# A six-stage decoder on one core: the first batch's memory attention moved into the last two expert units, with its loads and GpSimd's order rearranged

## What is computed

```python
# third sublayer (L0 ffn): 8 experts, capacity 1024 rows each
h = _rms(buf, norm_w[:, None, :])
gate = gelu(einsum('ech,ehf->ecf', h, Wg)); up = einsum('ech,ehf->ecf', h, Wu)
buf_out = einsum('ecf,efh->ech', gate * up, Wd) + buf
combined = x + contrib.reshape(N, TOP_K, H).sum(axis=1)      # or fout where a token overflows
...
# fourth sublayer (L1 attn), the "memory attention": M = 64
q, k, v = x @ Wq, x @ Wk, x @ Wv
gates = sigmoid(x @ Wg + bg)
S = decay * S + (k_t * g_t)[:, :, None] * (v_t * g_t)[:, None, :]
out_t = einsum('bd,bde->be', q_t, S);   y = outs @ Wo + bo
...
# fifth (L1 xattn): softmax attention over ctx_1024 with a mask; sixth (L1 ffn): 8 experts, all dense
```

## Time and profile before

| | us |
|---|---|
| Median of three runs | 1936.16 (1933.49 to 1940.54) |
| Profiled execution | 1936.2, span of its instructions 1934.4 |
| Mean granted TensorE clock, share of 2.4 GHz | 0.972 |
| TensorE busy | 1778.2 (92%) |
| VectorE, ScalarE, GpSimd busy | 1261.8, 991.2, 640.9 |

### The profile page before, as it was taken

One profiled execution on the slowest core, in us unless ns is written; L12 is line 12 of the kernel. 1 busy time (PEld: TensorE's weight loads), 2 busy tenths in 40 slices (PEclk: granted clock), 3 DMA queues, 4 the chain that ended last, 5 costly groups with the idle time before them and its releaser, 6 DMA issues. The chain is left out here.

```text
span 1934.4 us, 26137 instructions
## 1 busy us (share of the span) xinstructions
PE 1778.2 (92%) x8373; PEld 1056.8 (55%) x8373; DVE 1261.8 (65%) x2933; ACT 991.2 (51%) x2603; POOL 640.9 (33%) x821
## 2 busy tenths in 40 slices
PE   7999878899999898989889999999689999999997
PEld 5556534455555554545456556655455666566553
DVE  2686568898899999898411211221576878786665
ACT  4336699999999999896231111111242333233220
POOL 2000055555767676675410001000442323212100
PEclk9999989999999999999899999999788999999999
DMA  6248831122223222223653443332311111200000
GB/s 218 101 158 280 260 94 53 53 65 68 80 65 96 65 75 86 62 80 129 206 173 109 127 145 131 109 127 97 115 58 41 55 39 49 49 12 17 11 12 22
DMA packets 164072, 183.29 MB, mean 95 GB/s; under 512 B 19653, under 2 KB 143804, under 8 KB 162913
## 3 DMA queue, kind: packets, MB, share of 16 engines
q1 hardware_dynamic: 157792, 165.46, 27.0%
q0 software_dynamic: 6144, 16.18, 2.7%
HBM read 119.01 MB, written 63.18 MB: 94 GB/s over the span
## 5 line engine op out<-in xcount | busy, mean ns | idle before, releaser
L914 POOL TENSOR_SCALAR xa_probs<-xa_probs,xa_small 128x512 f32<-128x512 f32 x512 | 345.1, 691 | 227.6 <-DVE xa_small L1078 227.5
L987 ACT ACTIVATE xa_probs<-xa_ps_s,xa_small 128x512 f32<-128x512 f32 x512 | 363.6, 752 | 23.8 <-DVE xa_small L1084 20.1
L1084 DVE TENSOR_REDUCE xa_small<-xa_ps_s 128x2 f32<-128x1024 f32 x256 | 309.2, 1208 | 37.4 <-PE xa_ps_s L1355 37.4
L1368 PE MATMUL xa_ps_t<-xa_ident,xa_probs 128*128 128x128 f32 x2048 | 306.2, 283 | 13.7 <-DVE early L744 6.0
L1368 PEld LDWEIGHTS xa_ps_t<-xa_ident,xa_probs 128*128 128x128 f32 x2048 | 229.4, 142 | 147.1 <-ACT early L746 46.2
L2460 PE MATMUL ta_ps_e<-late,ta_x5T 128*128 128x512 f32 x512 | 235.8, 594 | 1.4 <-DVE ta_acc L2213 1.4
L1355 PE MATMUL xa_ps_s<-xa_k,xa_q 96*128 96x512 bf16 x496 | 151.1, 386 | 51.1 <-ACT xa_probs L987 51.0
L1624 ACT ACTIVATE ex_hid<-ex_ps_g 128x512 f32<-128x512 f32 x64 | 38.2, 597 | 270.2 <-PE ex_ps_u L1723 270.2
L2213 DVE SCALAR_TENSOR_TENSOR ta_acc<-ta_ps_e,ta_gate,ta_acc 128x256 f32<-128x256 f32 x256 | 123.5, 483 | 67.0 <-PE ta_ps_e L2460 60.8
L1679 DVE TENSOR_TENSOR ex_hid<-ex_hid,ex_ps_u 128x512 f32<-128x512 f32 x64 | 44.0, 688 | 180.2 <-ACT ex_hid L1624 180.2
L2460 PEld LDWEIGHTS ta_ps_e<-late,ta_x5T 128*128 128x128 f32 x512 | 93.9, 189 | 96.8 <-issue 83.3
(11 more groups left out here) (371 smaller groups left out, 3051.5 us busy)
## 6 DMA issues: line engine op xcount, KB each, us to landing
scratch_qk_parts<-front_w_all SPq DMA_DIRECT2D x16, 768.0 KB, 5.7
xa_q<-scratch_qk_parts SPq DMA_DIRECT2D x186, 64.0 KB
xa_k<-scratch_qk_parts SPq DMA_DIRECT2D x186, 64.0 KB
scratch_buf<-late SPq DMA_DIRECT2D x8, 1024.0 KB, 5.3
early<-in_L_ffn_Wg SPq DMA_DIRECT2D x16, 512.0 KB, 6.0
early<-in_L_ffn_Wu SPq DMA_DIRECT2D x16, 512.0 KB, 6.3
early<-in_L_ffn_Wd SPq DMA_DIRECT2D x16, 512.0 KB, 6.8
ex_xs<-scratch_buf SPq DMA_DIRECT2D x16, 512.0 KB, 5.2
```

The lines of the kernel that those rows point to most:

```text
L914: ins = pool.tensor_scalar(probs[n % NP][:, t, :], probs[n % NP][:, t, :], rinv[n % 2][:, t:t + 1], 1.0, ALU.mult, ALU.mult)
L987: ins = act.activation(probs[n % NP][:, t, :], ps_s[j][:, t % 2, :], ACT.Exp, bias=nmax[n % 2][:, t:t + 1], accum_out=rsum[n % 2][:, t:t + 1])
L1084: dve.tensor_reduce(nmax[n % 2][:, 2 * j:2 * j + 2], ps_s[j][:, :, :], AX.X, ALU.max, negate=True).then_inc(max_up, 1)
L1368: ins = pe.transpose(ps_t[t % 2][:, i * P:(i + 1) * P], probs[m % NP][:, i, t * P:(t + 1) * P], ident[:, :])
```

## The change

Three edits belong together.

1. *Memory attention of batch 0.* All its pieces leave step 0 of the tail and stand between the hidden blocks of units 14 and 15. They use ps_t, the PSUM tile of the turns, so the turn of unit 15 is made at the start of unit 14. Working tiles are laid over spent ones (x2, rows, z, fb). VectorE normalizes x4 of batch 0 after the last copy of the expert stage.
2. *Loads.* The norm weights of unit 15 are loaded apart, two units ahead. The first context goes to a tile `cT0` that outlives the stage; SP issues it behind the last store. The tail loads only the mask of batch 0, then x2, fallback and context of the next batches.
3. *The first step of the tail.* Step 0 is gone. In `first()` the context attention of batch 0 runs alone, with the combination of batch 1 on VectorE, and behind it the memory attention of batch 1. On GpSimd the gathers of batches 1 and 2 go first, separated by x4b of batch 0; then come x3b and risen of batch 1, the roots of zx of batch 0, of batch 2's combination and of batch 1, and behind these the gathers of batch 3. Steps 2 and later keep their order.

The diff, cut to its core:

```diff
@@ SP, experts
+                if m == NU - 4:
+                    sp.wait_ge(xsT_up, NU - 2)
+                    k.load_norm(sp, a, NU - 1, n_ld)
                 if m + 2 < NU:
                     k.load_expert(sp, a, m + 2, w_ld[m % 2])
+            sp.dma_start(k.cT0[:, :, :], a["ctxT"][0].rearrange("(h p) s -> p h s", p=P)).then_inc(k.cT0_ld, 16)
@@ GpSimd, experts
             pool.tensor_tensor(rstd[:, :], ve[:, :], k.mhalf[:, :], ALU.pow).then_inc(m_root, 1)
+            pool.wait_ge(m_x3, 1)
+            pool.tensor_tensor(x3b[:, :, :], k.x3[0][:, :, :], row(k.m_bo[:, :]).to_broadcast([P, T, D]), ALU.add).then_inc(m_x3b, 1)
+            pool.wait_ge(m_copy, 1)
+            pool.tensor_tensor(risen[:, :, :], qT[:, P:S].rearrange("p (t q) -> p t q", q=P),
+                               row(k.rise[:, :]).to_broadcast([P, T - 1, P]), ALU.mult).then_inc(m_risen, 1)
+            pool.wait_ge(b_var, 1)
+            pool.tensor_tensor(rb[:, :], veb[:, :], k.mhalf[:, :], ALU.pow).then_inc(b_root, 1)
@@ ScalarE, experts
+                if m == NU - 2:
+                    turn(NU - 1)
                 for j in range(FT):
...
+                    if (m, j) == (NU - 2, 0):
+                        act.wait_ge(m_t, 1)
+                        act.activation(x3T[:, :, :], ps_t[:, :, :], ACT.Copy).then_inc(m_xT, 1)
+                    if (m, j) == (NU - 2, 2):
+                        act.wait_ge(m_q, 1)
+                        act.activation(qT[:, :], ps_t[:, 0, :], ACT.Copy).then_inc(m_copy, 1)
+                        act.activation(k.kT[0:M, :], ps_t[M:2 * M, 0, :], ACT.Copy).then_inc(m_copy, 1)
+                    if (m, j) == (NU - 2, 3):
+                        act.wait_ge(m_v, 1)
+                        act.activation(g[:, :], ps_mgates, ACT.Sigmoid, bias=k.bg[:, 0:1]).then_inc(m_g, 1)
+                        act.activation(k.aged[:, :, 0:M], ps_mkeys, ACT.Copy, scale=k.fade[:, P - 1:P]).then_inc(m_aged, 1)
+                    if (m, j) == (NU - 1, 2):
+                        act.wait_ge(m_o, 1)
+                        act.activation(oT[:, :], ps_t[:, 0, :], ACT.Copy).then_inc(m_oT, 1)
@@ VectorE, experts
+                    if (m, j) == (NU - 2, FT - 1):
+                        gated()
+                    if (m, j) == (NU - 1, 0):
+                        carry()
+                    if (m, j) == (NU - 1, FT - 1):
+                        back()
...
+            dve.wait_ge(b_root, 1)
+            normalized(dve, k.x4, z2, mvb, rb)
@@ TensorE, experts
+                    if (m, j) == (NU - 2, 0):
+                        m_turn()
+                    if (m, j) == (NU - 2, 2):
+                        m_project()
+                    if (m, j) == (NU - 1, 0):
+                        m_outer()
+                    if (m, j) == (NU - 1, 2):
+                        m_reading()
-                if m + 1 < NU:
+                if m < NU - 2:
                     turn(m + 1)
+                if m == NU - 1:
+                    m_out()
...
                 for t in range(T):
+                    if (m, t) == (NU - 2, 2):
+                        m_scores()
@@ GpSimd, tail
+            sides(0)
             for u in range(2):
                 pool.wait_ge(k.result_st[u], 16 * E)
             gather(1)
+            with_bias(0)
+            gather(2)
+            pool.wait_ge(m_var, 1)
+            power(rm, vem, m_root)
...
-                if s_ == 0:
-                    pool.wait_ge(m_var, 1)
+                if s_ == 1:
+                    pool.wait_ge(x_var, 1)
+                    power(rx, vex, x_root)
+                    pool.wait_ge(m_var, 2)
                     power(rm, vem, m_root)
@@ VectorE, tail
+            def first():
+                m_front(1, 0)
+                m_front(1, 1)
+                x_maxima(0, 0)
+                x_maxima(0, 1)
+                m_front(1, 2)
+                m_front(1, 3)
+                x_maxima(0, 2)
+                m_front(1, 4)
+                x_out(0, 0)
+                m_front(1, 5)
+                x_maxima(0, 3)
+                x_out(0, 1)
+                m_front(1, 6)
+                x_out(0, 2)
+                x_out(0, 3)
+                x_norm(0)
+                combine(2)
+                m_gated(1)
+                m_faded(1)
+                m_carry(1)
+                m_front(2, 4)
+                m_front(2, 5)
+                m_front(2, 6)
+                m_back(1)
+                m_finish(1)
...
-            for s_ in range(B + 3):
+            for s_ in range(1, B + 3):
                 step(s_)
```

366 lines of the change are left out of this document (262 added, 104 removed).

## The result

| | median, us | runs | ratio to the kernel before, 95% |
|---|---|---|---|
| before | 1938.21 (1932.65 to 1945.77) | 20 | 1 |
| changed kernel | 1931.86 (1925.19 to 1940.60) | 20 | 0.9963 (0.9950 to 0.9975) |
| changed kernel, beside the experiments | 1931.03 | 12 | 0.9958 (0.9943 to 0.9974) |

A forecast was written before the change was run, and what follows sets the result against it. TensorE bounds the kernel, full except in the tail's first steps. Terms 9.2 + 6.5 + 14.1 + 21.4 + 2.5 + 9.4 + 16.3 + 20.5 + 13.3 = 113.2 against 116.7 us, so 1932.7 from 1936.2; 8-in-10 range 1922 to 1944.

The forecast's parts named there:

- Part 1: Expert units 14 and 15: batch 0's memory attention adds 9.2 us of TensorE pieces on the path; other engines' work costs nothing.
- Part 2: Last expert product to the first context's landing: TensorE waits 6.5 us, ends 5.5 and 9.
- Part 3: Batch 0's attention alone: context to first copied scores 14.1 us, then 21.4 to its last output row, plus 2.5 allowed.
- The allowance: 2.5 us added in batch 0's attention, before its last output row, for a stretch at half clock; ends 0 and 7.
- The slower rival: TensorE at 1.2 GHz through all of the tail's first step: 1943.7 us; chance 0.18.
- Part 4: Batch 1's memory attention behind batch 0: 9.4 us to its gates, then 16.3 to batch 3's gathers, at half clock.
- Part 5: Step 2: batch 3's late gathers, adds held by GpSimd; first gather to batch 2's gates 20.5 us, ends 15.1 and 21.
- The last term: Rest of step 2, to the first scores of batch 1's second attention: unchanged, 13.3 us.
- The sum: Last expert product to batch 1's first scores, plus the pieces moved into the units: 113.2 against 116.7 us, 3.5 less.
- The clock holds: TensorE stays at 2.4 GHz in the tail's first step: 8.8 us less, 1923.9 us; chance 0.18 together with earlier combination rows.
- The whole step 0 is gained: All 29.5 us of the tail's step 0 less 9.2 is saved: 20.3 us faster, 1916 us; chance 0.06.

The follow-up runs named there:

- hold: Changed kernel with GpSimd's four elementwise operations of step 2 held until VectorE has combined batch 3; ratio to the kernel before 0.9928.
- again: Second profiled execution of the same changed kernel, no edit; span 1934.7 us, last expert product to batch 1's first scores 100.2 us; ratio to before 0.9958.
- warm3: Changed kernel with unread idle TensorE products in pauses: around the tail's start and ahead of the outer products of batches 1 and 2; ratio to before 0.9913.
- interleaved: Changed kernel with the tail's first step in the old order, batch 1's memory attention interleaved with batch 0's second attention; ratio to before 1.0000.
- before_warm: Kernel before the change, with only idle TensorE products added in pauses of the tail's first steps; ratio to it 0.9965.
- early: Changed kernel with batch 3's gathers issued right after the tail's first root, GpSimd's four operations left directly behind batch 1's root; ratio to before 0.9941.
- warm_hold: Changed kernel with the edits of warm3 and hold, one idle product instead of five ahead of batch 2's outer products; ratio to before 0.9907.
- warm_hold2: warm_hold with four more idle products in step 2, around batch 0's turn and the router's turn and products; ratio to before 0.9920.

## Why the prediction was right, and where it was not

**Part 1, pieces in the units.** 9.2 forecast, 9.23 measured, 5.65 of it in unit 14 and 3.58 in unit 15. The sum of the single pieces gives this split too, with the 0.4 us for the turn that I had moved from the one unit to the other. The other engines' pieces and the table loads cost nothing that can be seen, as taken.

**Part 2, the context.** 6.5 forecast, 6.60 and 6.65 measured.

**Part 3.** Context to first copied scores 14.1 forecast, 14.2 and 13.8 measured. From there to the last output row 21.4 and an allowance of 2.5 forecast, 21.04 and 21.05 measured (1373.43 to 1394.47). The allowance was the term that failed: the clock did fall, but for 3.4 us in all (1377.3 to 1380.7), and the stretch was no longer for it. The slower rival, TensorE at 1.2 GHz through the whole step, falls with it. What I said of the clock and pauses from the earlier trace rows was also too narrow. The long pauses there were of 4.9 to 5.1 us. In the changed kernel the clock fell at 1377.3 behind a pause of 2.38 us. In the kernel before it fell at 1445.4, 0.3 us into a pause, and in the 17 us ahead of this pause TensorE had been idle for only 0.65.

**Part 4.** Last output row to the gates of batch 1: 9.4 forecast, 9.08 measured. Gates to the first gather of batch 3: 16.3 forecast, 15.4 and 15.7 measured. Up to the sum, at half clock as taken, it is 10.8 and 11.1 against 11.1; behind it 4.65 both times against 5.27, since GpSimd's root takes 1.01 us where it took 1.61 beside VectorE's mask of batch 0.

**Part 5.** First gather to the gates of batch 2: 20.5 forecast, 20.49 and 20.52 measured. I had taken the whole pattern of the earlier trace rows, and it came back to a tenth: eight adds in 8.94 us. *hold* shows its cause. Here the row decided against the rule of the Trainium skill (SBUF — State Buffer, Who interferes with whom), under which one side blocks the other for one instruction. That page says it of VectorE's modes that use two ports; for an operation with two inputs in SBUF, as these adds are, it only says that it contends with a GpSimd operation that reads SBUF. What decides is the first add, listed at 6.04 us over the rest of x3b, side, x4b and risen. The length of the pattern does not decide: the 1.2 us that I took off are about the time of three adds, which would run between GpSimd's operations, but under a lock each of them holds GpSimd up as long as it runs. The 5.8 us that GpSimd still had to run at 1430.62 and eight adds of 0.42 us make 9.1 us in any order (an estimate from these rows), against 8.94 measured. *hold* also has rows that fit the rule: the 128x32 operation from 1445.18 ends with GpSimd's x4b that it ran beside. What makes the adds wait for the whole run of GpSimd's operations, and these only for one, is open. One sign was off: TensorE's pause ahead of the outer products of batch 2 was 4.4 us and not 7.

**The last term.** 13.3 forecast; 10.97 and 13.32 measured. It is the clock again, which in one execution comes back ahead of the output product (1.99 instead of 3.78 us).

**The sum.** 113.2 forecast, 107.1 and 109.4 measured, so 9.6 and 7.3 us less than before instead of 3.5. Of the 6.1 us of error in the first execution 2.9 are part 3, 2.3 the last term and 0.9 the stretch of batch 1; in *again* 2.9 of 3.8 are part 3. The first two are terms where I took the rows at half clock, or an allowance for it, and the clock was better; of the third 0.6 is that root. The median, 1931.86, lies 0.8 below the forecast. That agreement is partly luck: the forecast starts from a median of 1936.16 out of three runs, and beside the changed kernel the kernel before took 1938.21, from which the same sum would have given 1934.7. Against its own neighbour the change gains 6 to 7 us (ratio 0.9963, which is 7.2), so the gain was twice what I forecast, with the right sign and the right mechanism; the mis-sized term was the allowance for the clock in part 3, 2.5 us of it with nothing measured.

**The rivals.** "The clock holds" did not happen by itself, except for one of its three terms: the allowance of 2.5 us was not needed. *warm3* gives the price of the other two. I had them at 2.3 us (values and turn) and 4.0 (gates to sum); *warm3* has 1.8 to 2.2 and 3.7 to 4.0. That its whole window lost 7.7 to 10.1 us is no confirmation of the 8.8: part of it is the last term, which the rival left out. "The whole step 0 is gained" falls twice: the changed kernel does not gain 20 us, and *interleaved*, which keeps the rest of the first step nearest to the old one, gains none.

## What to carry to other kernels

Work that is moved from a hole into a full stretch costs its whole TensorE time there; what it brings back depends on the order left in the hole, so the order behind the move is worth more thought than the move. Where a pause of TensorE stands ahead of work that others wait for, idle products in it can be worth as much as the change itself; where another engine sets the pace they are worth little. The windows of *before_warm* beside *warm3* show both; the timing alone would not. When an edit frees an engine, look for the next operation beside which the same work of GpSimd will lie: *early* moved a stall, and *hold* removed most of it.

## What was not expected of the hardware

- The clock can fall without a pause. In *warm_hold* the granted clock went from 1.00 to 0.50 at 1436 us, after 13.6 us in which TensorE was never idle for more than 0.22 us; the last pieces ahead of the fall were products with outputs of 128x130, 128x128 and 128x8. Wide idle products among them (*warm_hold2*) put it off by almost 4 us and did not prevent it. In *warm3* the same pieces were followed by ten instructions of idle products (4.5 us), and the clock stayed; but *warm3* had been at half clock until 1424 us, which *warm_hold* had not. *before_warm* has such a fall too, at 1445.1 us, with TensorE busy since 1428 us but for one pause of 0.65. What the difference rests on is open.
- A VectorE instruction of 0.17 us on 128x4 elements was listed at 3.95 us in *early*, and ended at 1408.98, when the second of two GpSimd operations ahead of it (the risen product, 1407.94 to 1408.95) did. It reads one tensor only, unlike the three in *hold*. So a stall of this kind is not bound to large tiles, nor to one GpSimd operation, nor to two inputs.
- The same kernel's spans differ by 10 us in two executions, and 7.3 us of it are there before the work that was moved begins, 5.6 already at the first expert product. A profiled pair of before and after can therefore agree or disagree with the timing by more than the change is worth.
